# A graph network with two expert layers: three row buffers instead of two in the second convolutions, and the experts' row numbers behind their weights

## The chip, the cores and the metric

The kernel runs on one core of a Trainium2 chip. The metric is the device time of one execution in microseconds (us), as the median over runs. TensorE is called PE below, VectorE DVE, ScalarE ACT, GpSimd POOL, and SyncE SP. SPq and ACTq are the sequencers of SP and ACT, where they issue DMAs.

## The reference

3125 nodes with 256 features each (padded to 3200 rows, 25 tiles of 128) go through four layers; each layer adds to x what it computes from the normalised x:

```
x = x + L0_gnn(layernorm(x))      # two SAGE convolutions, relu between them
x = x + L0_ffn(layernorm(x))      # 8 experts, the 2 best of each row, gelu
x = x + L1_gnn(layernorm(x))      # two SAGE convolutions again
x = x + L1_ffn(layernorm(x))      # a shared MLP and 4 small experts, 2 weighted
```

A convolution is `mean of the neighbours @ Wl.T + b + x @ Wr.T`. The edges (103,125, both directions and the loops) are the same in both graph layers. The kernel holds them as a matrix of counts, 3200 x 3200 in fp16, called `adj`.

## The kernel before, in words

The parts of the program follow one another: the first convolution of L0, the building of `adj` with the sums for the second, the second convolution of L0 (`second_conv`, tag `l_` in the rows), the experts of L0 inside it, the first convolution of L1, the second convolution of L1 (`second_conv` again, tag `l1b_`), and the last experts. The change touches `second_conv` and the place of one small tensor of `experts`.

`second_conv` has an early stage and a late stage. The early stage goes over the 25 row tiles k, and here is what each engine does for a tile:

- SP (`load(k)`, lines 1297 and 1301) loads the sums and z of the tile (256 KB) and the inverse degrees (64 KB) into one of the four slots of `ring`; it waits on `dense_done` of the tile that used the slot before. `load_x(k)` (line 1485) loads the tile's 128 x 256 residual rows (128 KB) into one of two buffers of `xb`, which lie in `room`; it first waits until the store of two tiles earlier has landed (`pre_out`).
- DVE (`neighbours(k)`, lines 1593 and 1595) scales the slot and adds to it, three tiles ahead of its own `take(k)` (lines 1599 and 1602). `take(k)` makes the low fp16 part of the product for `parts`, then adds the other half of the product to the residual rows in `xb`.
- ACT applies relu to the slot (line 1739, three tiles ahead), makes the high fp16 part (line 1749), and issues the store of `xb` to the DRAM tensor `pre` (`store_pre`, line 1743).
- PE does `dense(k)` (line 1809: the slot by the two weights, fp32, 2 matmuls that the trace records as 4) and `early(k)` (line 1833: the first ten output tiles' share of node tile k, 20 fp16 matmuls of 256 columns). Its order is dense(0), dense(1), early(0), dense(2), early(1), dense(3), and so on. The product banks are two, the sums of the ten tiles fill five banks.

All of it is written out by hand, in program order on each engine. A wait holds everything behind it on that engine. On SP the loop over k issues `load(k + 4)`, then `load_x(k + 2)`; so a load of a ring slot stands behind the wait for a store. At k = 6 SP also loads the first four row tiles of `pre` back (`load_rows(0)`, line 1488, 512 KB). On ACT, the high part of tile k + 1 stands behind the relu of tile k + 3, and the store of tile k comes right behind the high part of tile k + 1; the sequencer issues it as soon as it gets there.

The late stage takes the remaining 15 output tiles (line 1848), 50 matmuls each, with the normalisation and the gate between them. In L0 the experts follow. There ACT copies the row number out of every row that it takes (line 2166) into `ids`, and POOL reads it back (line 2201) for the scatter with addition.

Of the kernel before, what the change touches and what calls it, by code (L numbers as in the profile page):

```python
# [12 lines left out]
F32, F16, I32 = mybir.dt.float32, mybir.dt.float16, mybir.dt.int32  # L13
ALU = mybir.AluOpType
# [4 lines left out]
P = 128  # L19
D = 256  # L20
KD = D // P
NODES = 3125
TILES = -(-NODES // P)
# [28 lines left out]
E0, H0 = 8, 512  # L52
HB = H0 // P
ST = 256
STMAX = (2 * ROWS + E0 * (ST - 1)) // ST
# [1218 lines left out]
RING = 4  # L1274
# [65 lines left out]


EARLY_TILES = 2 * CT
LATE_BANKS = EARLY_TILES // 2 - 1


# [2 lines left out]
FINISHES = len(SIZES)  # L1348
MOST = max(SIZES)
# [36 lines left out]
def second_conv(nc, io, g, adj, parts, tag, names, gate, rows_from, rows_to, work, routing=False, final=None):  # L1386
# [4 lines left out]
    with ExitStack() as ctx:  # L1391
        pr = Prog(nc, ctx, tag)

        room, ring, w = work.room, work.ring, work.w
        xb = room[:, 2 * KD * D:].rearrange("p (u d) -> p u d", u=2)
        own = room[:, 0:KD * MOST * P].rearrange("p (f n) -> p f n", f=KD)

        split = lambda ap, shape, names: ap.rearrange(f"p ({names}) -> p {names}", **shape)
# [17 lines left out]
        if routing:  # L1416
# [6 lines left out]
            pre = pr.sb("pre", [P, MOST + 1, E], F32)  # L1423
# [4 lines left out]
            table = Route(nc, pr, g, room)  # L1428
# [4 lines left out]
            weights = expert_weights(parts)  # L1433
# [6 lines left out]
        dense_bank = [pr.ps(f"dense{i}", [P, 512]) for i in range(2)]  # L1440
        extra = pr.ps("extra", [P, 512])
        flat = room[0:E, KD * MOST * P:(KD + 1) * MOST * P]
        sum_bank = [pr.ps(f"sum{i}", [P, 512]) for i in range(EARLY_TILES // 2)]

# [1 line left out]
        last_bank = sum_bank[LATE_BANKS]  # L1446
        score_at, ranks_at, totals_at = (last_bank[:, at:at + MOST * E].rearrange("p (t e) -> p t e", e=E) for at in (0, 64, 128))
        s = {n: pr.sem(n) for n in (
            "final_in", "bias_in", "gate_in", "by_row_in", "x_in0", "x_in1", "pre_out0", "pre_out1", "h_sum", "h_done",
            "dense_done", "high_done", "low_done", "z_done", "agg_done", "sum_done", "x_out", "var_ready", "root_done",  # L1450
            "norm_done", "turned", "xt_ready", "xt_out", "multiplied", "flat_ready", "scored", "score_done", "consts", "pool_chain", "mask_ready",
            "ranked", "placed", "place_ready", "init", "chain", "route_chain", "hi_in", "hi_used")
            + tuple(f"in{r}" for r in range(RING)) + tuple(f"rows_in{c}" for c in range(FINISHES))
            + tuple(f"scattered{c}" for c in range(FINISHES))}
        block = ctx.enter_context(nc.Block())
        tiles_in = lambda c: slice(STARTS[c], STARTS[c + 1])
# [1 line left out]
        tile_of = lambda ap, k: ap[k * P:(k + 1) * P, :]  # L1458
# [9 lines left out]
            eng.wait_ge(table.s["dump_out"], 16)  # L1468

        if routing:  # L1470
            follow = experts(nc, io, g, pr, weights, ring, [*dense_bank, extra, *sum_bank], table, rows_placed)

        @block.sync
        def _(sp):
            def load(k):
                r = k % RING
                if k >= RING:
                    sp.wait_ge(s["dense_done"], k - RING + 1)
                work.load_sums(sp, k, s[f"in{r}"])
                work.load_inverse(sp, k, s[f"in{r}"])  # L1480

            def load_x(k):
                if k >= 2:
                    sp.wait_ge(s[f"pre_out{k % 2}"], 16 * (k // 2))
                sp.dma_start(xb[:, k % 2, :], tile_of(rows_from, k)).then_inc(s[f"x_in{k % 2}"], 16)

            def load_rows(c):
                sp.dma_start(rows_of(c), chunk_of(g["pre"], c)).then_inc(s[f"rows_in{c}"], 16)

            load_x(0)  # L1490
            load_x(1)
            for k in range(LOADED, RING):
                load(k)
            sp.dma_start(by_row[:, :], g["inv"].rearrange("a (t p) -> (a p) t", p=P), allow_slow_non_contiguous=True
                         ).then_inc(s["by_row_in"], 16)
            sp.dma_start(bias[:, :], io[b].rearrange("(a n) -> a n", a=1).broadcast_to([P, D])).then_inc(s["bias_in"], 16)
            sp.dma_start(wg[:, :, :], gate_w.rearrange("(k p) e -> p k e", p=P)).then_inc(s["gate_in"], 16)
            sp.dma_start(bg[:, :], gate_b.rearrange("(a e) -> a e", a=1).broadcast_to([P, E])).then_inc(s["gate_in"], 16)
            for k in range(TILES):
                if k + RING < TILES:  # L1500
                    load(k + RING)
                if k + 2 < TILES:
                    load_x(k + 2)
                if k == MOST + 2:
                    for u in range(2):
                        sp.wait_ge(s[f"pre_out{u}"], 16 * (MOST // 2))
                    load_rows(0)
            for u in range(2):
                sp.wait_ge(s[f"pre_out{u}"], 16 * ((TILES + 1 - u) // 2))
            sp.wait_ge(s["dense_done"], TILES)  # L1510
            for c in (1, 2, 6):
                load_rows(c)
            for c in (3, 4, 5):
                if routing:
                    sp.wait_ge(s[f"scattered{AFTER[c]}"], 16 * 2 * SIZES[AFTER[c]])
                sp.wait_ge(s["turned"], AFTER[c] + 1)
                load_rows(c)
            if final:


                sp.wait_ge(s["agg_done"], EARLY_TILES)
                final.load(sp, s["final_in"])
                sp.wait_ge(s["xt_out"], 16 * 2)
                final.load_rows(sp, 0, s["final_in"])
                sp.wait_ge(s["final_in"], 16 * (final.FIRST + final.SECOND + 1))
            if routing:
                sp.wait_ge(s["agg_done"], TILES)
                for e in range(2):
                    load_expert(sp, io, weights, e, e, table.s[f"first_w_in{e}"])
                table.clear(sp, 0, zero)  # L1530
                follow["sync"](sp)
# [53 lines left out]
        def _(dve):  # L1585
# [11 lines left out]
            def take(k):  # L1597
                dve.wait_ge(s["high_done"], k + 1)
                nc.vector.scalar_tensor_tensor(parts[:, k, 1, :], dense_bank[k % 2][:, 0:D], scale, parts[:, k, 0, :],  # L1599
                                               ALU.mult, ALU.subtract).then_inc(s["low_done"], 1)  # L1600
                dve.wait_ge(s[f"x_in{k % 2}"], 16 * (k // 2 + 1))
                nc.vector.tensor_tensor(xb[:, k % 2, :], dense_bank[k % 2][:, D:2 * D], xb[:, k % 2, :], ALU.add
                                        ).then_inc(s["z_done"], 1)

            def add_bias(c):
# [129 lines left out]
        def _(act):  # L1735
# [4 lines left out]

            def store_pre(k):
                act.wait_ge(s["z_done"], k + 1)
                act.dma_start(tile_of(g["pre"], k), xb[:, k % 2, :]).then_inc(s[f"pre_out{k % 2}"], 16)

            for k in range(RING - 1):
                relu(k)
# [14 lines left out]
            def take_turned(c):  # L1761
                act.wait_ge(s["turned"], c + 1)
                if c == 0:
                    for u in range(2):
                        act.wait_ge(s[f"pre_out{u}"], 16 * ((TILES + 1 - u) // 2))
                else:
                    act.wait_ge(s["multiplied"], c)
                    if not routing:
                        act.wait_ge(s["xt_out"], 16 * c)
                for f in range(KD):  # L1770
                    nc.scalar.activation(own[:, f, 0:SIZES[c] * P], dense_bank[f][:, 0:SIZES[c] * P], ACT.Copy
                                         ).then_inc(s["xt_ready"], 1)
                if not routing:
                    act.wait_ge(s["xt_ready"], KD * (c + 1))
                    act.dma_start(g["xt"][:, :, STARTS[c] * P:STARTS[c + 1] * P], own[:, :, 0:SIZES[c] * P]
                                  ).then_inc(s["xt_out"], 16)
# [166 lines left out]
    return take(2, KD, H0), take(2, HB, D), take(2, HB), take(2, D)  # L1943


def load_expert(eng, io, weights, e, u, sem):

    w1, w2, b1, b2 = weights
    for to, fr in ((w1[:, u, :, :], io["L0_ffn_W1"].rearrange("e (k p) h -> p (e k) h", p=P)[:, ds(e * KD, KD), :]),
                   (w2[:, u, :, :], io["L0_ffn_W2"].rearrange("e (k p) d -> p (e k) d", p=P)[:, ds(e * HB, HB), :]),  # L1950
                   (b1[:, u, :], io["L0_ffn_b1"].rearrange("e (k p) -> p (e k)", p=P)[:, ds(e * HB, HB)]),
                   (b2[:, u, :], io["L0_ffn_b2"][ds(e, 1), :].broadcast_to([P, D]))):
        eng.dma_start(to, fr, allow_slow_non_contiguous=True).then_inc(sem, 16)
# [84 lines left out]

def experts(nc, io, g, pr, weights, space, banks, table, rows_placed):

# [4 lines left out]
    NT = ST // P  # L2049
# [3 lines left out]
    def take(*shape):  # L2053
# [3 lines left out]
        return space[:, at:at + n].rearrange(f"p ({' '.join(names)}) -> p {' '.join(names)}", **dict(zip(names, shape)))  # L2057

    xt, h, y, xr = take(KD, ST), take(HB, ST), take(NT, D), take(NT, DW)
    ids = pr.sb("ids", [P, STMAX * NT], I32)  # L2060
    ids_now = pr.sb("ids_now", [P, NT], I32)
    px = banks[0][:, :].rearrange("p (k n) -> p k n", k=KD)
    ph = [banks[1 + n][:, 0:ST] for n in range(HB)]
# [1 line left out]
    s = {n: pr.sem("e_" + n) for n in ("w_in0", "w_in1", "w_free0", "w_free1", "rows_in", "turned", "xt_ready", "h_mm",  # L2065
                                       "h_done", "y_mm", "y_done", "ids_ready", "ids_now", "adding", "added")}
# [452 lines left out]
```

## Time and profile before

| | us |
|---|---|
| median of 3 runs | 1461.67 (1457.58 to 1467.45) |
| the profiled execution's own time | 1469.42 |
| its span | 1467.9 |
| PE busy | 1276.3 (87%) |
| DVE busy | 564.5 (38%) |
| ACT busy | 404.4 (28%) |
| POOL busy | 164.5 (11%) |

The span is that of the instructions in the profile; the profiled execution's own time is 1.5 us longer. The mean granted clock of PE is 0.943 of full speed. Matmuls are pipelined, so PE's busy share overstates how full it is.

### The profile page before, as it was taken

The page shows a single profiled execution, that of the slowest core. Times are in us where ns is not written, and L with a number is a line of the kernel's source. Part 1 is how long each engine was busy: PE and PEld are TensorE (multiplying, and loading weights), DVE is VectorE, ACT ScalarE, POOL GpSimd, SP SyncE. Part 2 cuts the span into 40 slices and gives each one's busy share as a digit, 9 for nine tenths or more (in the row PEclk, how much of TensorE's full clock was granted, in tenths as well). Part 3 has the DMA queues.
Part 4 walks back from the last instruction along what each step waited for, and adds up shares of the span by engine and source line. Part 5 has one row for each costly group of instructions (what it writes and reads, how often), then busy time and mean ns, then how long its engine had stood idle before and what let it go on. Part 6 is the DMA issues. An engine that isn't in the chain of part 4 may idle for free. (4 is left out here: it accounts for less than half of the span.)

```text
span 1467.9 us, 22148 instructions
## 1 busy us (share of the span) xinstructions
PE 1276.3 (87%) x7961; PEld 934.7 (64%) x7961; DVE 564.5 (38%) x1402; ACT 404.4 (28%) x811; POOL 164.5 (11%) x177
## 2 busy tenths in 40 slices
PE   3868999998998988199999829999899999989998
PEld 2547877775566766188888726655466678756665
DVE  5728777762345545200000044100043443343332
ACT  2344444431111101164446313200011110133333
POOL 2100000000000333334344400000000000000000
PEclk9888999999999988599999959999999999989999
DMA  5110000004543232535564432110055433150000
GB/s 163 61 50 1 16 17 16 16 8 123 150 140 107 71 100 83 172 58 113 119 131 69 87 83 90 52 58 26 27 139 146 123 135 101 58 183 18 18 34 18
DMA packets 132846, 116.55 MB, mean 79 GB/s; under 512 B 22595, under 2 KB 121284, under 8 KB 132770
## 3 DMA queue, kind: packets, MB, share of 16 engines
q1 hardware_dynamic: 100674, 74.19, 17.4%
q0 software_dynamic: 11984, 18.77, 6.5%
q10 hardware_dynamic: 20112, 22.56, 4.5%
q8 instruction: 51, 0.84, 0.2%
q14 instruction: 25, 0.20, 0.0%
HBM read 66.49 MB, written 48.99 MB: 79 GB/s over the span
## 5 line engine op out<-in xcount | busy, mean ns | idle before, releaser
L1203 PE MATMUL b_pa<-adj,l_parts 128*128 (+1 forms) x1100 | 144.6, 286 | 1.9 <-ACT ring L1126 1.9
L1141 ACT ACTIVATE adj<-b_pw 128x450 f32 (+1 forms) x176 | 87.1, 550 | 138.4 <-PE b_pw L1192 138.4
L1203 PEld LDWEIGHTS b_pa<-adj,l_parts 128*128 128x128 f16 x1100 | 105.6, 98 | 26.2 <-ACT adj L1141 2.0
L1032 DVE TENSOR_TENSOR ring<-b_it,key 128x1800 f16<-128x1800 f16 x88 | 96.2, 1094 | 45.9 <-PE b_pw L1192 44.9
L1192 PE MATMUL b_pw<-ring,room 128*128 128x150 f16 x1056 | 88.6, 236 | 25.9 <-DVE room L1032 24.9
L1593 DVE SCALAR_TENSOR_TENSOR ring<-ring,unscale 128x256 f32<-128x256 f32 x50 | 24.2, 484 | 221.8 <-PEq L106 147.9
L1848 PE MATMUL l_sum<-l_parts,adj 128*128 128x256 f16 x750 | 96.4, 288 | 14.1 <-issue 14.1
L2125 PE MATMUL l_sum<-l_parts,ring 128*128 128x256 f32 x448 | 104.2, 386 | 3.9 <-ACT ring L2170 0.6
L2184 DVE TENSOR_TENSOR ring<-l_sum,l_parts 128x512 f32<-128x512 f32 x28 | 19.4, 692 | 220.8 <-PE l_sum L2125 148.8
L1192 PEld LDWEIGHTS b_pw<-ring,room 128*128 128x128 f16 x1056 | 78.2, 101 | 33.2 <-DVE room L1032 30.2
L1848 PEld LDWEIGHTS l_sum<-l_parts,adj 128*128 128x128 f16 x750 | 75.4, 103 | 35.3 <-issue 23.3
L2125 PEld LDWEIGHTS l_sum<-l_parts,ring 128*128 128x128 f32 x448 | 82.8, 190 | 20.7 <-ACT ring L2170 9.7
L2206 POOL DMA_INDIRECT x<-ring,l_ids_now x56 | 86.7, 1547 | 61.6 <-DVE ring L2184 53.0
L1848 PE MATMUL l1b_sum<-l_parts,adj 128*128 128x256 f16 x750 | 86.4, 276 | 1.4 <-issue 1.4
L2376 ACT ACTIVATE l_parts<-m_bank,adj 128x320 f32<-128x320 f32 (+1 forms) x110 | 57.5, 526 | 105.6 <-PE m_bank L2340 46.3
L1032 DVE TENSOR_TENSOR room<-b_ib,low 128x1536 f16<-128x1536 f16 x88 | 83.7, 951 | 0.0
L1848 PEld LDWEIGHTS l1b_sum<-l_parts,adj 128*128 128x128 f16 x750 | 73.2, 99 | 14.9 <-issue 6.0
L1739 ACT ACTIVATE ring<-ring 128x256 f32<-128x256 f32 x50 | 20.8, 416 | 168.8 <-DVE ring L1595 168.8
L1833 PEld LDWEIGHTS l1b_sum<-l_parts,adj 128*128 128x128 f16 x500 | 48.8, 99 | 27.8 <-DVE l_parts L1599 15.9
L1833 PE MATMUL l1b_sum<-l_parts,adj 128*128 128x256 f16 x500 | 60.3, 278 | 5.5 <-DVE l_parts L1599 5.2
L1833 PEld LDWEIGHTS l_sum<-l_parts,adj 128*128 128x128 f16 x500 | 47.7, 98 | 27.4 <-DVE l_parts L1599 18.5
L1833 PE MATMUL l_sum<-l_parts,adj 128*128 128x256 f16 x500 | 58.7, 273 | 5.0 <-DVE l_parts L1599 4.9
(347 smaller groups left out, 1826.0 us busy)
## 6 DMA issues: line engine op xcount, KB each, us to landing
ring<-sums_and_zt SPq DMA_DIRECT2D x50, 256.0 KB, 3.4
l_parts<-in_L_ffn_W SPq DMA_DIRECT2D x16, 512.0 KB
ring<-slots_in SPq DMA_DIRECT2D x28, 257.0 KB
pre<-room ACTq DMA_DIRECT2D x50, 128.0 KB, 2.9
ring<-inv SPq DMA_DIRECT2D x50, 64.0 KB, 3.5
room<-in_x SPq DMA_DIRECT2D x25, 128.0 KB, 2.1
ring<-x SPq DMA_DIRECT2D x5, 640.0 KB, 6.5
sums_and_zt<-room ACTq DMA_DIRECT2D x5, 640.0 KB, 3.7
```

The costliest lines, as they stand in the source:

```text
L1032: return nc.vector.tensor_tensor(out.rearrange("p r (h two) -> p r h two", two=2), names[:, 0:width].rearrange("p (h two) -> p h two", two ...
L1141: ins = nc.scalar.activation(adj[:, :, ds(group * GW * W + b * BANKW * W, BANKW * W)].rearrange("p k (w j) -> p w k j", j=W), pw[u % SLOT ...
L1192: ins = nc.tensor.matmul(to, low[:, n, :], sel[:, n, :], start=i == 0, stop=i == VIS - 1)
L1203: ins = nc.tensor.matmul(pa[f][:, :], parts[:, k, a, f * P:(f + 1) * P], adj[:, k, ds(r * BW, BW)], start=k == 0 and a == 0, stop=k == TIL ...
L1593: ch.done(nc.vector.scalar_tensor_tensor(h[:, r, :, :], h[:, r, :, :], unscale, inv[:, r, :].unsqueeze(1).broadcast_to([P, KD, P]), ALU.mu ...
L1739: nc.scalar.activation(h[:, r, :, :], h[:, r, :, :], ACT.Relu).then_inc(s["h_done"], 1)
L1833: ins = nc.tensor.matmul(acc(t), adj[:, k, t * P:(t + 1) * P], parts[:, k, a, :], start=k == 0 and a == 0 and opens(t), stop=k == TILES - ...
L1848: ins = nc.tensor.matmul(acc(t), adj[:, k, t * P:(t + 1) * P], parts[:, k, a, :], start=k == 0 and a == 0 and opens(t), stop=k == TILES - ...
L2125: ins = nc.tensor.matmul(py[:, t, :], h[:, n, t * P:(t + 1) * P], w2[:, u, n, :], start=n == 0, stop=n == HB - 1)
L2184: nc.vector.tensor_tensor(y, py, b2[:, u, :].unsqueeze(1).broadcast_to([P, NT, D]), ALU.add).then_inc(s["y_done"], 1)
L2206: pool.indirect_dma_start(out=g["x1"], in_=y[:, t, :], in_offset=None, compute_op=ALU.add, out_offset=bass.IndirectOffsetOnAxis(ap=ids_now ...
L2376: nc.scalar.activation(to, fr, ACT.Relu, bias=bias).then_inc(s["act_took"], 1)
```

## The change

`xb` becomes three buffers: the two in `room` and a tensor of its own, `third` (128 x 256 fp32). Buffer, semaphore and wait go by k modulo 3. SP loads three row tiles ahead of its loop, and from the second pass on `load_x(k + 2)` stands where it stood, but waits on the store of tile k - 1 instead of tile k. The waits for all stores count three semaphores. In the experts, `ids` (128 x 64 int32) is no longer a tensor of its own: it lies in `l_parts` behind the experts' weights.

```diff
+XB = 3
-        xb = room[:, 2 * KD * D:].rearrange("p (u d) -> p u d", u=2)
+        third = pr.sb("third", [P, D], F32)
+        held = [room[:, (2 * KD + u) * D:(2 * KD + u + 1) * D] for u in range(2)] + [third[:, :]]
+        xb = lambda k: held[k % XB]
+        uses = lambda u: len(range(u, TILES, XB))
...
             def load_x(k):
-                if k >= 2:
-                    sp.wait_ge(s[f"pre_out{k % 2}"], 16 * (k // 2))
-                sp.dma_start(xb[:, k % 2, :], tile_of(rows_from, k)).then_inc(s[f"x_in{k % 2}"], 16)
+                if k >= XB:
+                    sp.wait_ge(s[f"pre_out{k % XB}"], 16 * (k // XB))
+                sp.dma_start(xb(k), tile_of(rows_from, k)).then_inc(s[f"x_in{k % XB}"], 16)
...
-            load_x(0)
-            load_x(1)
+            for k in range(XB):
+                load_x(k)
             for k in range(LOADED, RING):
                 load(k)
...
             for k in range(TILES):
                 if k + RING < TILES:
                     load(k + RING)
-                if k + 2 < TILES:
-                    load_x(k + 2)
+                if 1 <= k and k + XB - 1 < TILES:
+                    load_x(k + XB - 1)
...
+WEIGHTS_SIZE = 2 * (KD * H0 + HB * D + HB + D)
+def ids_place(parts):
+    room = parts[:, :, :, :].rearrange("p t a d -> p (t a d)").bitcast(I32)
+    return room[:, WEIGHTS_SIZE:WEIGHTS_SIZE + STMAX * (ST // P)]
...
-    ids = pr.sb("ids", [P, STMAX * NT], I32)
+    ids = ids_place(parts)
```

SP at the head of the second convolution of L0, before (`room<-in_x` is a row load into `xb`, `ring<-sums_and_zt` and `ring<-inv` are the load of one ring slot):

```order
66 L1485 DMA room<-in_x 128x256 x2
67 L1297 DMA ring<-sums_and_zt 128x4x128
68 L1301 DMA ring<-inv 128x128
69 L1297 DMA ring<-sums_and_zt 128x4x128
70 L1301 DMA ring<-inv 128x128
71 L1494 DMA l_by_row<-inv 128x25x1
72 L1496 DMA l_bias<-in_L_gnn_b 128x256
73 L1497 DMA l_gate_w<-in_L_ffn_Wg 128x2x8
74 L1498 DMA l_gate_b<-in_L_ffn_bg 128x8
75 L1297 DMA ring<-sums_and_zt 128x4x128
76 L1301 DMA ring<-inv 128x128
77 L1485 DMA room<-in_x 128x256
```

The same place after the change:

```order
66 L1489 DMA room<-in_x 128x256 x2
67 L1489 DMA l_third<-in_x 128x256
68 L1297 DMA ring<-sums_and_zt 128x4x128
69 L1301 DMA ring<-inv 128x128
70 L1297 DMA ring<-sums_and_zt 128x4x128
71 L1301 DMA ring<-inv 128x128
72 L1498 DMA l_by_row<-inv 128x25x1
73 L1500 DMA l_bias<-in_L_gnn_b 128x256
74 L1501 DMA l_gate_w<-in_L_ffn_Wg 128x2x8
75 L1502 DMA l_gate_b<-in_L_ffn_bg 128x8
76 L1297 DMA ring<-sums_and_zt 128x4x128
77 L1301 DMA ring<-inv 128x128
```

The third row load now stands ahead of the ring slots 2 and 3 (rows 67 to 71), where before it stood behind slot 0's second load (row 77).

DVE at the third `take` of the same stage, before and after (`room` or `l_third` is the row buffer of the tile):

```order
187 L1599 SCALAR_TENSOR_TENSOR l_parts<-l_dense,scale,l_parts 128x256
188 L1602 TENSOR_TENSOR room<-l_dense,room 128x256
189 L1593 SCALAR_TENSOR_TENSOR ring<-ring,unscale 128x256
```

```order
187 L1603 SCALAR_TENSOR_TENSOR l_parts<-l_dense,scale,l_parts 128x256
188 L1606 TENSOR_TENSOR l_third<-l_dense,l_third 128x256
189 L1597 SCALAR_TENSOR_TENSOR ring<-ring,unscale 128x256
```

Only the buffer's name differs; nothing moved on DVE, and eight of the 25 tiles of a stage go through `third`.

## Rows read from the trace of the kernel before

**Rows 1.** The page, its first line

```profile
span 1467.9 us, 22148 instructions
```

**Rows 2.** Windows, both early stages: busy us (x instructions) by engine, clock, DMA share, GB/s

```profile
353.20:450.20 97.00, 92.01 (x554) 59.61 (x554) 40.02 (x92) 17.63 (x45) 0.00 (x0) 1.00 0.49 140
...
1070.50:1168.80 98.30, 93.03 (x553) 60.77 (x554) 39.67 (x92) 17.74 (x45) 0.00 (x0) 0.98 0.49 139
```

**Rows 3.** Waits, 350 to 455 us, and the last row 1065 to 1172 us

```profile
DVE ring L1593 <- DMA ring<-inv: 35.7, 21, 3.3
...
PE l_sum L1833 <- DVE l_parts L1599: 4.9, 9, 0.9
...
SPq L1485 <- DMA pre<-room: 58.1, 23, 3.6
...
SPq L1485 <- DMA pre<-room: 58.5, 23, 4.0
```

**Rows 4.** Timeline of PE: start, length, instructions of some `early` steps

```profile
353.20 2.36 PE L1833 MATMUL l_sum<-l_parts,adj 128*128 128x256 f16 x20
...
361.20 2.36 PE L1833 MATMUL l_sum<-l_parts,adj 128*128 128x256 f16 x20
...
417.49 2.35 PE L1833 MATMUL l_sum<-l_parts,adj 128*128 128x256 f16 x20
...
421.39 2.35 PE L1833 MATMUL l_sum<-l_parts,adj 128*128 128x256 f16 x20
...
450.14 4.53 PE L1833 MATMUL l_sum<-l_parts,adj 128*128 128x256 f16 x40
...
1070.52 2.36 PE L1833 MATMUL l1b_sum<-l_parts,adj 128*128 128x256 f16 x20 [0.29 <-DVE l_parts L1599]
...
1078.52 2.36 PE L1833 MATMUL l1b_sum<-l_parts,adj 128*128 128x256 f16 x20
...
1168.77 4.53 PE L1833 MATMUL l1b_sum<-l_parts,adj 128*128 128x256 f16 x40
```

**Rows 5.** Timeline, one trip from a store to the store two tiles on

```profile
386.42 0.33 ACTq L1743 DMA_DIRECT2D pre<-room  x1
...
390.30 0.33 SPq L1485 DMA_DIRECT2D room<-in_x  x1
...
391.27 0.62 SPq L1301 DMA_DIRECT2D ring<-inv  x1
...
394.91 0.48 DVE L1593 SCALAR_TENSOR_TENSOR ring<-ring,unscale 128x256 f32<-128x256 f32 x1 [2.14 <-DMA ring<-inv]
...
395.90 0.33 ACTq L1743 DMA_DIRECT2D pre<-room  x1
...
397.25 2.36 PE L1833 MATMUL l_sum<-l_parts,adj 128*128 128x256 f16 x20 [0.86 <-DVE l_parts L1599]
```

**Rows 6.** Lines 1743 (store) and 1301 (inverse degrees), issue to landing

```profile
DMA to landing us min/median/max: 1.7/2.9/4.2
...
DMA to landing us min/median/max: 3.1/3.5/5.0
```

**Rows 7.** Timeline, second convolution of L1, around the load of rows 0

```profile
1100.03 1.62 SPq L1488 DMA_DIRECT2D l1b_rows<-pre  x1
...
1109.27 4.02 PE L1833 MATMUL l1b_sum<-l_parts,adj 128*128 128x256 f16 x20 [2.46 <-DVE l_parts L1599]
```

**Rows 8.** Windows, the same place: columns as in rows 2

```profile
1110.00:1112.00 2.00, 2.00 (x12) 1.43 (x10) 1.16 (x3) 0.78 (x2) 0.00 (x0) 0.50 0.39 114
```

**Rows 9.** Timeline, head of the second convolution of L0

```profile
345.76 0.82 SPq L1485 DMA_DIRECT2D room<-in_x  x2
...
347.22 0.62 SPq L1301 DMA_DIRECT2D ring<-inv  x1
...
350.87 0.49 DVE L1593 SCALAR_TENSOR_TENSOR ring<-ring,unscale 128x256 f32<-128x256 f32 x1 [3.25 <-DMA ring<-inv]
```

**Rows 10.** Line 2166, ACT's copies of the row numbers: ns min/median/max

```profile
L2166 ACT ACTIVATE l_ids<-ring x28: 196/197/198, 620.2 to 830.0; 128x2 f32 x28
```

More of the change, by code:

```diff
@@ L1448, in second_conv @@
         s = {n: pr.sem(n) for n in (
-            "final_in", "bias_in", "gate_in", "by_row_in", "x_in0", "x_in1", "pre_out0", "pre_out1", "h_sum", "h_done",
+            "final_in", "bias_in", "gate_in", "by_row_in", "h_sum", "h_done",
             "dense_done", "high_done", "low_done", "z_done", "agg_done", "sum_done", "x_out", "var_ready", "root_done",
@@ L1452, in second_conv @@
             "ranked", "placed", "place_ready", "init", "chain", "route_chain", "hi_in", "hi_used")
-            + tuple(f"in{r}" for r in range(RING)) + tuple(f"rows_in{c}" for c in range(FINISHES))
+            + tuple(f"x_in{u}" for u in range(XB)) + tuple(f"pre_out{u}" for u in range(XB)) + tuple(f"in{r}" for r in range(RING)) + tuple(f"rows_in{c}" for c in range(FINISHES))
             + tuple(f"scattered{c}" for c in range(FINISHES))}
@@ L1470, in second_conv @@
         if routing:
-            follow = experts(nc, io, g, pr, weights, ring, [*dense_bank, extra, *sum_bank], table, rows_placed)
+            follow = experts(nc, io, g, pr, parts, weights, ring, [*dense_bank, extra, *sum_bank], table, rows_placed)
         @block.sync
@@ L1501, in _ @@
                     load(k + RING)
-                if k + 2 < TILES:
-                    load_x(k + 2)
+                if 1 <= k and k + XB - 1 < TILES:
+                    load_x(k + XB - 1)
                 if k == MOST + 2:
-                    for u in range(2):
-                        sp.wait_ge(s[f"pre_out{u}"], 16 * (MOST // 2))
+                    for u in range(XB):
+                        sp.wait_ge(s[f"pre_out{u}"], 16 * len(range(u, MOST, XB)))
                     load_rows(0)
-            for u in range(2):
-                sp.wait_ge(s[f"pre_out{u}"], 16 * ((TILES + 1 - u) // 2))
+            for u in range(XB):
+                sp.wait_ge(s[f"pre_out{u}"], 16 * uses(u))
             sp.wait_ge(s["dense_done"], TILES)
@@ L1600, in take @@
                                                ALU.mult, ALU.subtract).then_inc(s["low_done"], 1)
-                dve.wait_ge(s[f"x_in{k % 2}"], 16 * (k // 2 + 1))
-                nc.vector.tensor_tensor(xb[:, k % 2, :], dense_bank[k % 2][:, D:2 * D], xb[:, k % 2, :], ALU.add
+                dve.wait_ge(s[f"x_in{k % XB}"], 16 * (k // XB + 1))
+                nc.vector.tensor_tensor(xb(k), dense_bank[k % 2][:, D:2 * D], xb(k), ALU.add
                                         ).then_inc(s["z_done"], 1)
@@ L1742, in store_pre @@
                 act.wait_ge(s["z_done"], k + 1)
-                act.dma_start(tile_of(g["pre"], k), xb[:, k % 2, :]).then_inc(s[f"pre_out{k % 2}"], 16)
+                act.dma_start(tile_of(g["pre"], k), xb(k)).then_inc(s[f"pre_out{k % XB}"], 16)
             for k in range(RING - 1):
@@ L1763, in take_turned @@
                 if c == 0:
-                    for u in range(2):
-                        act.wait_ge(s[f"pre_out{u}"], 16 * ((TILES + 1 - u) // 2))
+                    for u in range(XB):
+                        act.wait_ge(s[f"pre_out{u}"], 16 * uses(u))
                 else:
@@ L2037, in vector, with experts @@
         dve.wait_ge(s["tables_ready"], 1)
-def experts(nc, io, g, pr, weights, space, banks, table, rows_placed):
+def experts(nc, io, g, pr, parts, weights, space, banks, table, rows_placed):
     NT = ST // P
```

## The prediction

> **What bounds the kernel now.** I read the page first for where the two stages that the change touches lie in the span of 1467.9 us [rows 1], then the windows over these stages, then the waits there with the DMA queue's own among them, then the timeline. The reader is to see in the windows that the two early stages are 97.0 and 98.3 us long, that PE is busy for about 95% of each, and that the DMA engines are busy for half of the time (share 0.49) [rows 2]. So PE is nearly the bound, but not quite. PE's busy time is modelled and hides small gaps, so the period of a tile says more. Where nothing holds PE up, one `early` starts 3.90 us after the one before (417.49 to 421.39), which is one `early` and one `dense` back to back. Over the stages the period is longer: 353.20 to 450.14 holds 23 periods, 96.94 us or 4.21 each; 1070.52 to 1168.77 holds 23 periods too, 98.25 us or 4.27 each [rows 4]. At 3.90 each, 23 periods are 89.7 us. The waste of PE in the two stages is 7.2 and 8.5 us, together 15.8, and no edit of the buffers can give more.
>
> Who holds it? PE waits for DVE's low part, DVE waits most for the ring slot's inverse degrees, 35.7 us in 21 waits; and the issuer of these loads, SP, waits 58.1 and 58.5 us for stores to land, 23 times per stage, in its own row load (line 1485) [rows 3]. One trip of this loop can be read in the timeline [rows 5]. ACT issues the store of a tile at 386.42. The row load of two tiles on, held by it, goes out at 390.30. Behind it on SP stands the ring load, whose second DMA goes out at 391.27. DVE has it at 394.91 and needs 0.99 us until ACT gets past the relu and issues the next store but one at 395.90; the `early` behind it starts at 397.25, after PE had stood idle for 0.86 us. That trip covers two tiles in 9.48 us, where PE needs 2 x 3.90 = 7.80. With the median landings, 2.9 us for a store and 3.5 for the inverse degrees [rows 6], a trip is 2.9 + 0.97 (row load to ring load) + 3.5 + 0.99 = 8.36 us, 4.18 per tile. That is the period measured. So the loop through two buffers bounds both stages, by about 0.3 us per tile, and everything else of the kernel is outside it.
>
> **The change part by part.**
>
> The wait. With three buffers the same trip runs from a store to the store three tiles on. PE needs 3 x 3.90 = 11.70 us for these, the trip 8.36. Even both landings at their longest, 4.2 and 5.0 [rows 6], make 4.2 + 0.97 + 5.0 + 0.99 = 11.16, still below 11.70. So PE is late next, at 3.90. What else could be late: SP's other wait, for `dense_done` before a ring load. It lets slot 0 be loaded when dense(k) ends, and the relu of tile k + 4 must be through before the high part of tile k + 2, which is two periods or 7.8 us later. The ring load needs about 0.6 us for the issue of the sums ahead of it, 3.5 for the landing and 0.99 for DVE and ACT, 5.1 together; 2.7 remain. Behind the high part PE still has an `early` and a `dense` to do, 3.90 us, of which 397.25 - 395.90 = 1.35 are used by the high and low part. So a landing can be more than 5 us late before PE sees it. DVE (about 40 us busy of 97) and ACT (18 of 97) [rows 2] have room. Gain: 23 x 3.90 instead of 96.94 and 98.25, so 7.2 and 8.5 us.
>
> The head. The third row load is issued ahead of the ring slots 2 and 3, and the first `early` hangs on slot 2: its load goes out at 347.22 and reaches DVE at 350.87. Two row loads take 0.82 us to issue, so the third takes 0.41 [rows 9]. It has no cover on DVE's side, as DVE and ACT waited for slot 2. I take 0.41 per stage, 0.8 in all. It can be 0 if `dense`, which ends at the moment at which the first `early` starts, gives the pace, and about 1 us per stage if the 128 KB also delay the landing. The next two tiles depend on loads that stand behind the bias and gate loads. Tile 2 starts at 361.20, 0.20 after 353.20 + 7.80, and in L1 at 1078.52, also 0.20 after 1070.52 + 7.80 [rows 4]. No store is waited for there, so these 0.20 stay, 0.4 in all.
>
> The rows loaded back in the middle. In L1, SP spends 1.62 us on issuing them, the ring load behind is late, PE stands 2.46 us and then its clock is at 0.50 of full speed, 1.2 GHz, for some 2 us: the `early` after it takes 4.02 instead of 2.36 [rows 7, 8]. The pause and the slow clock, 2.46 + 1.66, are 4.1 us. With the slack above this lateness is covered too. But in L0 the same load took no such time, so it does not belong to every execution.
>
> The stage ends. Behind the last `early`, the high part waits only for PE itself and all later work hangs on the last tile. I take it that both stages shift what follows by their whole gain.
>
> The row numbers. The 28 copies on ACT take 197 ns each [rows 10], 5.5 us in all. Same shape, same engine, another address: 0. The bounds are plus and minus the whole of them, 5.5, but no reason for either is in the trace, and the value nearest to the row is no change. The third buffer on DVE and for the DMAs likewise differs in its address alone. Four more semaphores in all to clear at the ends: 0 to 0.5 us.
>
> The sum against the profiled execution: 15.8 - 0.8 - 0.4 = 14.6 us, 1469.4 to 1454.8. That execution was 7.7 us over the median of the runs, 1461.67, and the pause with its slow clock, 4.1 us, may be a part of this. Without it the gain is 14.6 - 4.1 = 10.5. I take the middle, 12.5: 1461.67 - 12.5 = 1449.2 us.
>
> **The rivals.** First: all of the waste comes back, in a usual execution as in the profiled one. For it speaks that every piece of slack above is over 2 us. Against it, that landings scatter. 14.6 to 16 us, about 1446.5.
>
> Second: the ring loads stay late, because store, row load and ring load now overlap where they had been in a row. Half of the gaps stay: 7 us, about 1455. For it: the DMA engines are busy half of the time and a landing takes longer beside others (5.0 at most against 3.1 [rows 6]). Against it: bytes per tile are the same, and the share rises only from 0.49 to 0.49 x 97.0 / 90.1 = 0.53.
>
> Third: nothing happens, since the wait moves whole to the ring slots. SP's 58 us become a wait on `dense_done` and the slots are filled no earlier. Then only the head is paid: 1462.5. Against it: in the trip above 3.88 us pass on SP between the store and the row load [rows 5], and the slot was free all the time.
>
> Fourth, slower: the loads and the store that now run together stretch each other, and the trip over three tiles becomes longer than three of today's periods. Today's mean is (96.94 + 98.25) / 46 = 4.24 us, so the point is 12.73 us per trip, or 10.8 for the two landings against 6.4 by the medians and 9.2 by the longest. Past it, at 13.2 (4.40 per tile), the cost is 46 x 0.16 = 7 us: about 1469. The place is SP's row load and the ring load behind it.
>
> The Trainium skill, in "DMA: Bandwidth & Descriptors", section "Issuing engines are not separate DMA queues", says that transfers issued by different engines all run on the same 16 DMA engines and interleave. That rule is what the fourth rival rests on; the trace has the landings of 3.1 to 5.0 us beside it, which agree with sharing, but at a share of a half it shows no queue that is full.
>
> **How the numbers follow.** A measurement of this kernel tells about 1% (14.6 us) from no change. Chances: the forecast, a gain of 9 to 14.5 us, 0.40; all of it, 14.6 or more, 0.30; half, 0.18; nothing, 0.07; slower, 0.05. So faster by over 1% has 0.30, within 1% 0.65 and slower 0.05. The range runs from 1443 (all of the waste and the scatter of a median) to 1457.5 (half of the gain with scatter to the other side). The likeliest case's own range is 1447 to 1453.
>
> **What would show it.** Right: `early` steps 3.90 us apart nearly throughout both stages, so 90.5 us from the first to the step of 40 matmuls; the first `early` 0.4 us later after the stage's start; SP's wait for stores down from 58 to under 20 us, with part of it now a wait for `dense`; DVE's wait for the inverse degrees smaller or gone; no half clock inside the L1 stage; late stages and experts as long as before. Wrong: gaps before `early` that stay with the ring load as their cause (second rival), periods of 4.2 us (third), landings of over 5 us as the rule (fourth), or a late stage that grows by what the early one gave.

## The result, and the profile after

The changed kernel takes 1440.05 us (median of 4 runs, 1437.92 to 1443.04), the kernel before 1459.62 us in the 4 runs that stand beside it (1455.75 to 1467.45). The ratio is 0.9873 with a 95% interval of 0.983 to 0.9916. Two later comparisons of the same pair give 0.9895 (0.9855 to 0.9936) and 0.9888 (0.9843 to 0.9933). Each ratio is an estimate over the fast runs of both kernels and not the quotient of the two medians. By the ratios the change brings 15 to 19 us, more than the 12.5 of the prediction; the medians of the three pairs lie 18.5 to 19.6 us apart. The time lies below the range, which ended at 1443.

The windows over the two early stages of the changed kernel answer to [rows 2]; the columns are the same:

```profile
350.50:440.50 90.00, 89.91 (x552) 60.62 (x553) 37.55 (x93) 19.60 (x45) 0.00 (x0) 1.00 0.55 151
1045.90:1135.90 90.00, 89.90 (x552) 60.61 (x553) 37.36 (x92) 19.59 (x45) 0.00 (x0) 1.00 0.54 150
```

PE is busy throughout (89.9 of 90.0 us), and its clock is full in both stages. The same work is done in 7 and 8 us less, so the DMA share rises from 0.49 to 0.55 and 0.54. In the timeline of PE, the steps that answer to [rows 4]:

```profile
350.56 2.36 PE L1837 MATMUL l_sum<-l_parts,adj 128*128 128x256 f16 x20 [0.59 <-DVE l_parts L1603]
...
358.57 2.36 PE L1837 MATMUL l_sum<-l_parts,adj 128*128 128x256 f16 x20
362.48 2.35 PE L1837 MATMUL l_sum<-l_parts,adj 128*128 128x256 f16 x20
...
440.53 4.53 PE L1837 MATMUL l_sum<-l_parts,adj 128*128 128x256 f16 x40
...
1045.89 2.36 PE L1837 MATMUL l1b_sum<-l_parts,adj 128*128 128x256 f16 x20
...
1135.93 4.53 PE L1837 MATMUL l1b_sum<-l_parts,adj 128*128 128x256 f16 x40
```

From the first `early` to the step of 40 matmuls it is 89.97 and 90.04 us, where it was 96.94 and 98.25. That is 23 periods of 3.91. The third tile starts 0.21 us after 350.56 + 7.80, as before. From there nothing holds PE up.

The waits answer to [rows 3], in the same window of the second convolution of L0. The first three rows are SP's, the fourth is DVE's:

```profile
SPq L1297 <- PE l_dense L1813: 20.7, 15, 1.8
SPq L1489 <- DMA pre<-room: 18.6, 14, 3.6
SPq L1489 <- DMA pre<-l_third: 8.5, 6, 3.5
...
DVE ring L1597 <- DMA ring<-inv: 5.4, 3, 2.8
```

SP's wait for stores is 27.1 us instead of 58.1, and 20.7 us of waiting are now for `dense`, that is for a free ring slot. DVE waits for the ring 5.4 us instead of 35.7. A turn like that in [rows 5] can be read in four rows of the new timeline:

```profile
389.99 0.55 SPq L1297 DMA_DIRECT2D ring<-sums_and_zt  x1
...
390.00 0.33 ACTq L1747 DMA_DIRECT2D pre<-room  x1
...
393.38 0.33 SPq L1489 DMA_DIRECT2D room<-in_x  x1
...
393.89 0.55 SPq L1297 DMA_DIRECT2D ring<-sums_and_zt  x1
```

The ring load at 389.99 leaves at the moment at which the store leaves, and not behind its landing. The row load waits 3.38 us for the landing, but is over in time for the next ring load, one period of PE later.

The spans of the two profiles differ by more than the times, 1467.9 against 1436.4. Cut at the same instructions, the 31.5 us divide like this (us, before minus after):

| part | before | after | difference |
|---|---|---|---|
| start to first `dense` of L0 | 347.25 | 344.10 | 3.15 |
| L0, first `dense` to the 40 matmuls | 102.89 | 96.43 | 6.46 |
| L0, the 40 matmuls to the last ranks | 144.37 | 125.60 | 18.77 |
| experts, first convolution of L1 | 469.95 | 473.22 | -3.27 |
| L1, first `dense` to the 40 matmuls | 104.31 | 96.58 | 7.73 |
| from there to the end | 299.13 | 300.47 | -1.34 |

The two rows of the stages that the change touches give 14.2. The late stage of L0 gives 18.8 that no step of the prediction has. In the profile of before, PE does single matmuls there with pauses for which no releaser is seen:

```profile
499.54 0.27 PE L1848 MATMUL l_sum<-l_parts,adj 128*128 128x256 f16 x1 [0.45 <-issue]
...
521.00:525.00 4.00, 4.00 (x21) 2.74 (x20) 2.31 (x13) 0.00 (x0) 0.00 (x0) 0.50 0.49 131
...
PE l_sum L1848 <- issue: 14.1, 22, 2.1
```

The next single matmul comes at 500.25, the one after it at 500.95. The second row is a window, with the columns of [rows 2]: behind the pauses of 517 to 521 us the clock is 0.50 of full speed, 1.2 GHz, and the 21 matmuls take 4.00 us. In the changed kernel's profile the last of these rows reads 5.7 us in 2 times. The pauses are only about half of the difference: PE is busy for 121.1 us of this stage before and for 110.7 after, at mean clocks of 0.89 and 0.95. Whether this belongs to the kernel or to one execution was the first question to the chip.

### The profile page after: what moved, and what is told of

Its sections match the earlier page's. It is cut to its first block and busy times, and to the rows that moved or that the text cites. A ratio compares the mean times of both kernels' runs of the same rounds, so it can differ in the third digit from the quotient of the medians.

```text
span 1436.4 us, 22152 instructions
## 1 busy us (share of the span) xinstructions
PE 1261.2 (88%) x7961; PEld 933.2 (65%) x7961; DVE 559.0 (39%) x1402; ACT 408.0 (28%) x811; POOL 164.2 (11%) x177
## 3 DMA queue, kind: packets, MB, share of 16 engines
q0 software_dynamic: 11984, 18.77, 6.7%
## 5 line engine op out<-in xcount | busy, mean ns | idle before, releaser
L1852 PE MATMUL l_sum<-l_parts,adj 128*128 128x256 f16 x750 | 86.6, 276 | 5.7 <-issue 5.7
L1852 PE MATMUL l1b_sum<-l_parts,adj 128*128 128x256 f16 x750 | 86.0, 275 | 1.5 <-issue 1.5
L1852 PEld LDWEIGHTS l_sum<-l_parts,adj 128*128 128x128 f16 x750 | 73.2, 99 | 19.6 <-issue 10.5
L1837 PEld LDWEIGHTS l1b_sum<-l_parts,adj 128*128 128x128 f16 x500 | 48.7, 98 | 19.6 <-issue 12.6
L2445 DVE SCALAR_TENSOR_TENSOR adj<-m_bank,m_weight,adj 128x256 f32 x100 | 42.6, 478 | 48.1 <-PE m_bank L2360 48.1
L462 PE MATMUL n_agg<-adj,l_parts 128*128 128x448 f16 (+1 forms) x300 | 60.6, 361 | 0.0
L1837 PE MATMUL l_sum<-l_parts,adj 128*128 128x256 f16 x500 | 58.5, 273 | 0.6 <-DVE l_parts L1603 0.6
```

What stands on the lines that cost most here:

```text
L462: ins = nc.tensor.matmul(pairs[n % 3][f][:, 0:size], parts[:, k, a, f * P:(f + 1) * P], moving, start=start and a == 0, stop=stop and a == 1)
L1837: ins = nc.tensor.matmul(acc(t), adj[:, k, t * P:(t + 1) * P], parts[:, k, a, :], start=k == 0 and a == 0 and opens(t), stop=k == TILES - ...
L1852: ins = nc.tensor.matmul(acc(t), adj[:, k, t * P:(t + 1) * P], parts[:, k, a, :], start=k == 0 and a == 0 and opens(t), stop=k == TILES - ...
```

## The experiments

**The kernel before once more, for a second profile.** Nothing was edited.

> The kernel before, unchanged, for a second profile. Open after the first comparison: of the 31.5 us between the two spans only 15 lie in the two early stages; 18.5 lie in the late stage of L0 (end of the 40 early matmuls' start to the last small matmul: 144.4 us before, 125.7 after), where PE in the profile of before does single matmuls 0.7 us apart for some 16 us. Theory A (that stutter is chance of one execution): here the late stage of L0 is well below 144 us, 125 to 138, and the span nearer 1457. Theory B (it belongs to the kernel before): 144 us again and the stutter again. Early stages in both: 96 to 99 us from first early to the step of 40.

The span was 1464.1 us and the late stage of L0 124.9 us (455.27 to 580.19). The waits of PE there:

```profile
PE l_sum L1848 <- issue: 5.1, 2, 3.7
```

The stutter is gone from the same kernel, so Theory A holds for it: it is not in every execution of the kernel before. In the eight other profiles of the study, with either form of the early stages, the late stage takes 121.2 to 125.6 us. The expected span, nearer to 1457, was missed, as other parts of this execution were longer: from the last ranks of L0 to the first `dense` of L1 it took 480.0 us, where the first profile had 469.95. 23 runs of this kernel in that comparison lay between 1445 and 1470. The early stages took 98.71 and 98.85 us, more than in the profile that the prediction was made from.

**The row numbers alone.**

```diff
-    ids = pr.sb("ids", [P, STMAX * NT], I32)
+    ids = ids_place(parts)
```

> Row numbers behind the experts' weights, still two row buffers. Theory A (the gain is the buffers'): ratio 0.998 to 1.002, early stages 96 to 99 us. Rival (the freed tensor or its place matters for something): ratio below 0.997.

Ratio 1.0017 (0.9987 to 1.0047); early stages 97.32 and 99.34 us. Theory A, though the second stage is 0.3 us over its bound: this edit moves no time that can be measured, and the interval leaves room for 2 us less to 7 us more. It makes room: the third buffer beside the old `ids` does not fit into SBUF, so there is no run of the buffer alone with the old `ids`.

**Three buffers with the old wait.**

```diff
                 if k >= XB:
-                    sp.wait_ge(s[f"pre_out{k % XB}"], 16 * (k // XB))
+                    sp.wait_ge(s[f"pre_out{(k - 2) % XB}"], 16 * ((k - 2) // XB + 1))
```

> Three buffers, but the row load of tile k waits for the store of tile k - 2, as with two. Theory A (the wait on the store is the whole of it): early stages back at 96 to 99 us, SP waits about 58 us for stores in each, ratio 0.998 to 1.003 (the third load ahead costs 0.4 to 0.8 us). Rival (three buffers help in another way, or the late stage's gain comes with them): ratio near 0.990 or lower.

Ratio 1.0021 (0.9993 to 1.0048); early stages 97.84 and 99.00 us. SP's waits in the L0 stage:

```profile
SPq L1489 <- DMA pre<-room: 41.9, 15, 4.5
SPq L1489 <- DMA pre<-l_third: 17.7, 7, 3.0
```

They add up to 59.6 us, where two buffers had 58.1. Theory A: a third buffer brings nothing that can be measured while the wait is the old one. The gain comes with the new wait.

**The changed kernel in more rounds.**

> The changed kernel, unchanged, in more rounds and on the same chip as the two others. Theory A (15 us in the early stages and nothing that lasts elsewhere): ratio 0.989 to 0.991. Theory B (the late stage of L0 gives several us of its own in every execution): ratio 0.985 to 0.988. In its profile early stages of 90 us.

Ratio 0.9895 (0.9855 to 0.9936), medians 1439.84 and 1458.43; stages of 90.18 and 90.11 us. The ratio lies in Theory A's figures, but its interval holds nearly all of Theory B's too, so the time alone can't tell them apart. The profile does: the late stage of L0 takes 125.1 us with the new wait, and 123.4 to 124.9 in the three later profiles with the old one. Over the four profiles with the old wait the two stages take 195.2, 197.6, 196.7 and 196.8 us together, over the four with the new wait and three buffers 180.0, 180.3, 179.9 and 179.8. The means are 196.6 and 180.0. Less 1 us or so at the heads, that is 15.6 us, and 1458.4 - 15.6 = 1442.8, a ratio of 0.9893. That lies inside the interval of every comparison. The medians lie 3 to 4 us further apart than this. The profiles can't place these: the stretch from the last ranks of L0 to the first `dense` of L1 alone takes 470 to 481 us in the ten profiles of the study, with either wait. Whether they belong to the change is not shown.

**The wait for the store of one tile earlier.** Two buffers; a trip then covers one tile.

```diff
                 if k >= 2:
-                    sp.wait_ge(s[f"pre_out{k % 2}"], 16 * (k // 2))
+                    sp.wait_ge(s[f"pre_out{(k - 1) % 2}"], 16 * ((k - 1) // 2 + 1))
```

> Two buffers, but the row load of tile k waits for the store of tile k - 1. It tests the length of the trip. Theory A (a trip of about 8.4 to 8.6 us, from a store over the row load and the ring load behind it to the store that it lets through, sets the period; before, it covers two tiles): now it covers one, so 8.4 to 8.6 us per tile, the step from the first early to the 40 matmuls 193 to 198 us in each stage where it was 98, and 190 to 200 us more in the whole: 1650 to 1660. Rival (the store's wait is only one of several things that hold the stage up): clearly under 170 us per stage.

1572.94 us, one run. The stages grew to 154.7 and 152.8 us, 6.7 per tile: so the expectation of Theory A is missed by some 40 us per stage, and the stages lie under 170, where the rival had put them. One trip of the timeline says which part of Theory A was off:

```profile
408.93 0.33 ACTq L1743 DMA_DIRECT2D pre<-room  x1
...
410.64 0.33 SPq L1485 DMA_DIRECT2D room<-in_x  x1
...
411.61 0.62 SPq L1301 DMA_DIRECT2D ring<-inv  x1
...
414.81 0.48 DVE L1593 SCALAR_TENSOR_TENSOR ring<-ring,unscale 128x256 f32<-128x256 f32 x1 [1.70 <-DMA ring<-inv]
...
415.79 0.33 ACTq L1743 DMA_DIRECT2D pre<-room  x1
```

The trip has the form that was expected, and its 6.86 us are close to the mean period of 6.7. But the store lands within 1.71 us and not 2.9. Here nothing else is under way when it leaves, and lines 1743 and 1301 have these landings (least, median, most):

```profile
DMA to landing us min/median/max: 1.7/1.7/4.2
...
DMA to landing us min/median/max: 3.1/3.3/5.1
```

With the medians the trip is 1.7 + 0.97 + 3.3 + 0.99 = 6.96. The form of the loop is shown, as no second thing that holds the stage up is needed for the 6.7. What was wrong is the length of a trip: it is no constant, as the landings in it change with the order and the moments of issue.

**Two buffers, ring load first.** The ring load is taken out from behind the wait.

```diff
+            load(RING)
             for k in range(TILES):
-                if k + RING < TILES:
-                    load(k + RING)
+                if k + RING + 1 < TILES:
+                    load(k + RING + 1)
                 if k + 2 < TILES:
                     load_x(k + 2)
```

> Two row buffers as before, but on SP the load of ring slot k + 5 stands ahead of the row load of tile k + 2, so that no ring load stands behind a wait for a store of its own turn. Theory A (what costs is the ring load behind the wait, not the number of row buffers): early stages of 90 to 92 us from first early to the step of 40, head of 6.0 us instead of 6.5, ratio 0.988 to 0.991, as the changed kernel or half a microsecond to one better. Rival (the rows themselves come too late with two buffers): DVE waits for rows ahead of line 1602 and the stages stay at 94 to 98 us, ratio 0.994 to 1.

Ratio 0.9869 (0.982 to 0.9919), 1438.43 us against 1441.86 of the changed kernel on the same chip. The stages take 89.95 and 90.18 us, the heads 5.90 and 6.05. Theory A: two buffers are enough if the ring loads don't stand behind the store. DVE waits more for rows, as the rival has it, 7.7 us in the L0 stage where the kernel before had 3.4, but that wait stays off PE's path:

```profile
DVE room L1603 <- DMA room<-in_x: 7.7, 8, 1.6
```

**The third row load later at the head.**

```diff
-            for k in range(XB):
+            for k in range(2):
                 load_x(k)
             for k in range(LOADED, RING):
                 load(k)
+            load_x(2)
```

> The changed kernel with the third row load behind the loads of ring slots 2 and 3 at the head. Theory A (that load delays the first early by 0.4 to 0.5 us per stage): from the first dense to the first early 6.0 us instead of 6.5, stages of 90 us, 1 us less in all than the changed kernel, which the timing hardly tells. Rival (the head's 0.5 us come from elsewhere): 6.5 again.

From the first `dense` to the first `early` it takes 5.97 us in both stages, where the changed kernel beside it took 7.03 and 6.37. Stages of 90.04 and 89.79 us. Theory A for the head. The ratio, 0.9864 (0.9818 to 0.991), can't tell half a microsecond.

**The changed kernel beside the two.**

> The changed kernel on the same chip as ring_first and third_later. Both theories: ratio 0.987 to 0.991; stages of 90 us. It is the measure for the two.

Ratio 0.9888 (0.9843 to 0.9933); stages of 89.80 and 90.12 us. The three kernels are the same as far as these runs can tell. Ring load first needs the least SBUF and no move of the row numbers.

## Why the prediction was wrong where it was wrong

**The bound and the loop: right.** The period fell from 4.21 and 4.27 to 3.91, PE is late next, SP's wait turned in part into one for `dense`, and the half clock in L1 is gone. It is absent from the three later profiles with the old wait too, so it was no fixed part of the waste. SP's wait for stores stayed at 27.1 us, where under 20 was forecast. The old wait with three buffers and the shifted ring load with two show from both sides that the ring load behind the wait was the cause.

**The head: right in place, a little small.** 0.41 per stage was taken; it is 6.46 - 5.95 = 0.5 and 6.54 - 6.06 = 0.5 in the first profile, and 0.4 to 1.1 in the pair that ran beside each other.

**The row numbers and the slack: right.** Landings of ring loads rose from 3.5 to 3.8 us in the median, which the slack hides. Landings of stores fell from 2.9 to 1.7. That goes against the fourth rival and the second. The store in [rows 5] left 0.4 us after the second half of a ring load (issued at 386.01), and the row load that waited for it went out 3.88 us later; in the kernel with the wait of one tile it leaves alone and lands in 1.7. The Trainium skill says, in "DMA: Bandwidth & Descriptors", section "Issuing engines are not separate DMA queues", that transfers of different issuers run on the same 16 DMA engines and interleave; these two landings agree with that. But in the changed kernel the store leaves 0.01 us behind the first half of a ring load (390.00 and 389.99 above), and the median landing is 1.7 too, so company alone does not make it long.

**The step that failed: the end of the sum.** The sum against the profiled execution was 14.6 us, and the runs show 15.6. The prediction cut it to 12.5, because that execution was 7.7 us over the median and a pause with its slow clock, 4.1 us, "may be a part of this". It was not. In three more profiles with the old wait the two stages together are 1.5 to 2.4 us longer than in the profiled execution, not shorter. The surplus of that execution lay in the late stage of L0, which took 19 to 23 us more than in the other nine profiles; that it was only 7.7 us over the median fits with the stretch behind it, which was 7 to 10 us shorter than in the three later profiles with the old wait. The late stage showed it in the waits of PE, as 14.1 us for "issue" where the second profile of this kernel has 5.1, and it was not looked at.

**The base.** The forecast started from 1461.67, the median of three runs. With 4, 11 and 23 runs the same kernel has 1459.6, 1460.4 and 1458.4. About 2 us of the miss are this: 1461.67 - 1440.05 is 21.6, of which 15.6 are the stages. Of the rest, 1.3 to 3.3 us are the base. The others, 2.7 to 4.7, are found in no stage; they may be the scatter of a median of 4 runs, but the later pairs have some 3 us of the same sign, so this part stays open. The range ended below at 1443 with too little room for these. Even with 15.6 in the sum the forecast would have been 1446.1. The likeliest case was said to be a gain of 9 to 14.5 us; it was the first rival, the whole waste.

## What to carry to other kernels

A wait in a queue is paid by everything behind it. Ask of a loop which load that is on the path stands behind a wait that is not, and try the order of issue before another buffer: here it gave the same. Before a sum is cut because the profiled execution was slow, find the place where that execution was slow.

## What was not expected of the hardware

The landing of a store of 128 KB is 1.7 us in the median where it leaves alone (the wait of one tile) and also where it leaves at the same moment as a ring load (the changed kernel), but 2.9 in the kernel before, where it left 1 us behind the first half of a ring load in [rows 5]. So a loop that is bound by such trips got shorter ones when it was slowed down: one trip of 6.86 us, where the medians of the kernel before give 8.36. Which of the transfers ahead of a store stretches it was not tested. And in one execution of ten PE did matmuls of 0.27 us some 0.7 us apart in four places of the late stage of L0, with no releaser in the profile; about half of the 19 us lie in longer busy time, partly at a clock of 0.50. What it came from is open; no run was made for it. It showed in one of the five profiles with the old wait or the wait of one tile and in none of the five with the new order, which is too few to say that it is as frequent in both.
